# Softmax scaling moved from VectorE to ScalarE, and deferred output products drained two at a time, in an attention and FFN kernel on eight cores

## The reference

```
q_c, q_r = xn @ Wq, rope(xn @ Wqr)          # 16 heads, 64 + 32 features
latent   = xn @ Wkvd                        # 256 features
k_c, v   = latent @ Wku, latent @ Wvu;  k_r = rope(xn @ Wkr)
scores   = [q_c, q_r] . [k_c, k_r] / sqrt(96), causal
e        = exp(scores - m);  attn = e / (sum(e) + exp(lobo_log))
y        = (attn @ v) @ Wo
h        = fix(pwl_gelu(fix(xn @ w1 + b1))) # 4096 features, rounded to 1/256
out      = x + y + fix(h @ w2 + b2)
```

## Time and profile before

| what | value |
|---|---|
| median of 3 runs | 4929.59 us (4919.1 to 4930.2) |
| profiled execution | 4929.35 us |
| its span, slowest core (core 4) | 4927.5 us |
| spans of the eight cores | 4886.9 to 4927.5 us |
| busy: VectorE, TensorE, ScalarE | 50%, 42%, 23% of the span |
| granted TensorE clock, mean | 0.645 of full speed |

### The profile page before, as it was taken

The page is one execution under the profiler, slowest core; times in us unless marked ns, Lnnn a source line. Parts: engine busy times, 40 slices in busy tenths (PEclk is TensorE's granted clock), DMA queues, the critical chain, the costliest instruction groups (busy, mean ns, idle before and its releaser), DMA issues.

```text
span 4927.5 us, 37045 instructions; the slowest of 8 cores (4886.9 to 4927.5 us)
## 1 busy us (share of the span) xinstructions
PE 2056.3 (42%) x7010; PEld 817.0 (17%) x7072; DVE 2455.7 (50%) x4454; ACT 1137.9 (23%) x1957; POOL 386.8 (8%) x352
## 2 busy tenths in 40 slices
PE   0111026035444534444445445455544455454545
PEld 0000002011111111111111122222222222222221
DVE  1222231048755765675582555555555555555551
ACT  1111001011111211111110333333333333333320
POOL 1000000012211211221120000000000000000001
PEclk8555558556676666657655566666666666666668
DMA  5222320942233222222222344444444444444454
GB/s 96 58 58 62 96 62 9 107 73 55 56 73 72 54 66 68 64 57 71 71 56 74 65 81 76 82 77 80 76 82 76 81 77 77 79 81 79 79 91 67
DMA packets 883113, 352.69 MB, mean 72 GB/s; under 512 B 831824, under 2 KB 834384, under 8 KB 882384
## 3 DMA queue, kind: packets, MB, share of 16 engines
q1 hardware_dynamic: 871184, 309.89, 29.8%
q0 software_dynamic: 11712, 40.44, 6.3%
HBM read 174.68 MB, written 41.94 MB: 44 GB/s over the span
## 4 chain that ended last, share of the span: by engine, by line
DMA 31%; DVE 23%; PE 20%; issue 12%; ACT 6%; another core or an unknown queue 3%; SPq 2%; DVEq 1%; ACTq 0%; POOL 0%; POOLq 0%
DMA PT<-Ebuf 10%; DMA W2C<-w2bf 7%; DMA W1C<-w1bf 6%; PE ps L659 6%; DVE u_t L917 6%; PE ps L998 4%; PE ps L631 3%; DMA xtile<-xb 2%; ACT Ebuf L904 2%; DVE Ebuf L948 2%; PE ps L809 2%; PE ps L874 2%; DMA out<-OB 1%; PE ps L496 1%
## 5 line engine op out<-in xcount | busy, mean ns | idle before, releaser
L917 DVE TENSOR_REDUCE u_t<-Ebuf 128x1 f32<-128x1536 bf16 (+3 forms) x480 | 644.8, 1354 | 338.6 <-ACT Ebuf L904 337.8
L904 ACT ACTIVATE Ebuf<-ps 128x1536 bf16<-128x1536 f32 (+3 forms) x480 | 544.8, 1136 | 943.0 <-DVE ps L892 815.2
L659 PE MATMUL ps<-xnTq,W1C 128*128 128x512 bf16 x1006 | 439.7, 612 | 758.7 <-DMA W1C<-w1bf 756.6
L874 PE MATMUL ps<-kasm,qh 96*128 96x512 bf16 (+1 forms) x1152 | 445.7, 499 | 630.2 <-ACT Ebuf L904 609.8
L998 PE MATMUL ps<-PT,vtok 128*64 128x256 bf16 x2304 | 451.2, 381 | 334.8 <-DMA PT<-Ebuf 332.1
L631 PE MATMUL ps<-W2C,HQ 128*128 128x512 bf16 x1001 | 353.6, 496 | 319.3 <-DMA W2C<-w2bf 116.3
L998 PEld LDWEIGHTS ps<-PT,vtok 128*64 128x64 bf16 x2304 | 350.9, 158 | 480.6 <-issue 422.8
L675 ACT ACTIVATE FT<-ps,b1t 128x512 f32<-128x512 f32 x128 | 88.0, 687 | 1458.4 <-PE ps L659 1458.4
L892 DVE TENSOR_TENSOR ps<-ps,m12sb 128x128 f32<-128x128 f32 x512 | 123.8, 288 | 373.9 <-PE ps L874 373.9
L691 DVE TENSOR_SCALAR FT<-FT 128x512 f32<-128x512 f32 x128 | 55.6, 434 | 503.6 <-ACT FT L675 503.3
L659 PEld LDWEIGHTS ps<-xnTq,W1C 128*128 128x128 bf16 x1024 | 130.3, 136 | 1047.0 <-issue 1044.2
(11 more groups left out here) (93 smaller groups left out, 2169.3 us busy)
## 6 DMA issues: line engine op xcount, KB each, us to landing
W2C<-w2bf SPq DMA_DIRECT2D x256, 256.0 KB, 2.8
W1C<-w1bf SPq DMA_DIRECT2D x128, 256.0 KB, 3.4
xtile<-xb SPq DMA_DIRECT2D x32, 512.0 KB, 4.0
xtile<-xq SPq DMA_DIRECT2D x16, 512.0 KB, 4.0
out<-xtile SPq DMA_DIRECT2D x16, 512.0 KB, 3.0
w1bf<-w POOLq DMA_DIRECT2D x8, 1024.0 KB, 48.4
w2bf<-w POOLq DMA_DIRECT2D x8, 1024.0 KB, 122.3
out<-FT POOLq DMA_DIRECT2D x16, 512.0 KB, 5.4
```

What stands on the lines that cost most here:

```text
L659: ins = e.matmul(bkh, W1C[:, fc % 2, dc, :], XNQ[:, dc, tg * 512:(tg + 1) * 512], start=(dc == 0), stop=(dc == 7))
L874: ins = e.matmul(PS[:, (tb + m) * 512:(tb + m) * 512 + wd], QH[0:96, hp, oi * 128:(oi + 1) * 128], KA[0:96, hp, gs + m * 512:gs + m * 512 ...
L904: return e.activation(EB[:, slotE, gs:gs + gl], PS[:, tb * 512:tb * 512 + gl], AF.Exp, scale=SCALE96, accum_out=u_t[:, ub + gi:ub + gi + 1])
L917: ub=ub, gi=gi: e.reduce_max(u_t[:, ub + 3 + gi:ub + 4 + gi], EB[:, slotE, gs:gs + gl], axis=AX.X)),
```

## The change

There are two edits. In the FFN each chunk takes up to two products out of the queue instead of three. In attention the multiplication of a row by its reciprocal leaves VectorE: `fred` ends with the reciprocal and increments a new semaphore `s_fr`, and an Identity activation on ScalarE with the reciprocal as scale does the multiplication. Both rows' activations, and both transposes, are written after all of the pair's exponentials and ahead of the read-out L1007 and of the next pair's exponentials.

```
-            drain_o(3)
+            drain_o(2)
...
-                def fred(e, slotE=slotE, km=km, ng=len(grps), h=h, ub=ub):
+                def fred(e, km=km, ng=len(grps), h=h, ub=ub):
...
-                    vhz(e, e.reciprocal(u_t[:, r8 + 9:r8 + 10],
-                                        u_t[:, r8 + 8:r8 + 9]))
-                    return e.tensor_scalar(EB[:, slotE, 0:km],
-                                           EB[:, slotE, 0:km],
-                                           u_t[:, r8 + 9:r8 + 10], None,
-                                           ALU.mult)
+                    return e.reciprocal(u_t[:, r8 + 9:r8 + 10],
+                                        u_t[:, r8 + 8:r8 + 9])
                 ev("vector", fred, waits=[s_sex, s_gmx] +
...
-                    else []), incs=[(s_red, 1)])
+                    else []), incs=[(s_fr, 1)])
+                rowq.append((slotE, km, ub, s_fr.n))
                 if rr == 0:
                     ev("vector", (lambda e, kmA=KMU[oiA], kmB=KMU[oiB], k=k:
                                   e.memset(EB[:, (2 * k) % 3, kmA:kmB], 0.0)),
...
+            red_rr = []
+            for slotE_, km_, ub_, frn_ in rowq:
+                ev("scalar", (lambda e, slotE=slotE_, km=km_, ub=ub_:
+                              e.activation(EB[:, slotE, 0:km],
+                                           EB[:, slotE, 0:km], AF.Identity,
+                                           scale=u_t[:, ub + 9:ub + 10])),
+                   waits=[(s_fr, frn_)], incs=[(s_red, 1)])
+                red_rr.append(s_red.n)
+            rowq.clear()
...
+            for rr in range(2):
                 ev("sync", (lambda e, rr=rr, K=Kb, k=k, pto=pto: e.dma_start(
                     out=PT[:, pto:pto + K, rr * 128:rr * 128 + 128],
...
-                   waits=[s_red, (sp, sp.n)] +
+                   waits=[(s_red, red_rr[rr]), (sp, sp.n)] +
                    ([(s_pv, pv_pr[k - 2])] if k >= 2 else []),
                    incs=[(sp, 16)])
```

More of the change, by code:

```diff
@@ L216, in build_program @@
     s_gmx = sem("gmx")
+    s_fr = sem("fr")
     s_etp = [sem("etrA", dma=True), sem("etrB", dma=True)]
@@ L794, in build_program @@
     pend_pv = [None]
+    rowq = []
     smm_hd, vtr_hd, pv_hd = {}, {}, {}
@@ L959, in build_program @@
                        incs=[(s_red, 1)])
-                Kb = KMU[oiB] // 128
-                pto = 0 if k % 2 == 0 else 28
-                sp = s_etp[k % 2]
+            red_rr = []
[7 more added lines that the diff above has]
+            rowq.clear()
+            Kb = KMU[oiB] // 128
+            pto = 0 if k % 2 == 0 else 28
+            sp = s_etp[k % 2]
+            for rr in range(2):
                 ev("sync", (lambda e, rr=rr, K=Kb, k=k, pto=pto: e.dma_start(
```

## The result

The changed kernel takes 5195.46 us (median of 8 runs, 5189.77 to 5207.35) against 4929.89 us (8 runs, 4917.05 to 4938.96) in the same comparison: ratio 1.0544, 95% interval 1.0529 to 1.0559, or 266 us slower. The forecast was 5233, the range 5050 to 5330.

A forecast was written before the change was run, and what follows sets the result against it. No attention engine was full; VectorE worked almost unbroken for 101.1 of a head's 127.25 us, and w2 loads on SyncE's queue chained long FFN chunks. 4929.35 + 386 (attention) - 82 (FFN) = 5233 us, range 5050 to 5330.

The forecast's parts named there:

- The walk through a head: Attention, pair by pair with scalings on ScalarE: pair 7 takes 23.5 us instead of 17.68; sixteen heads +386 us.
- the boundary: Between two heads, 26.1 us before: row B's transpose lands 10.0 us after the last scaling instead of 6.9, +3.1.
- The order costs more than the price: Attention: late scalings, queued ahead of exponentials, and late transposes cost more than ScalarE's 2.07 us for the mean row.
- the lost run-ahead: Attention: ScalarE no longer runs the next row's first exponentials while VectorE combines and scales; no separate size.
- the serial transposes: Attention: both transposes of a pair start late, one after the other, 6.1 us each for 3584 columns.
- The lower bound of +13 a head for a cheap activation: Attention with activations at VectorE's price: still about +13 us a head (+208), as successive transposes set row B's start.
- a stall: FFN, wait at emit_foq, two a group: with two products a chunk each costs some 6 us over two chunks.
- nearly neutral: FFN: averaging three-product and one-product chunks gives 12.2 us against 12.0 for two-product chunks, so hardly any gain.
- VectorE's queue as the bound (faster): Rival, attention: VectorE bounds a head, which loses just its VectorE scalings, 12.6 us; 4646 us, chance 0.10.
- The FFN without gain: Rival, FFN: the read-out blocks VectorE for 14 us and the saving is lost again in waits; 5315 us, chance 0.14.
- Table loads: Rival, attention: Identity between exponentials needs table loads, 256 adding 328 us; 5561 us, chance 0.04 shared with the upper price.
- The lower price in attention: Rival: ScalarE's activations at about VectorE's speed, +208 in attention; 5055 us, chance 0.12 shared with milder ordering.

The follow-up runs named there:

- the half-row run: The changed kernel with ScalarE's scaling activation on only the first half of each row's columns, the other half left unscaled: 5073.48 us, ratio 1.0311.

## Why the prediction was right

**The sum.** +386 and -82 were forecast, +304; 266 us were measured, 38 less. The two experiments with one edit each give +364 and -88, so attention was put 22 us too high and the FFN's gain 6 us too low. The other 10 us, 0.2% of the time, lie between the sum of the two single edits and both together; no run explains them.

**The walk through a head.** It held step by step. Pair 7: 23.5 us forecast, 23.8 measured; row B's exponentials free at 9.3, in fact 10.1; both transposes landed 10.0 after the last scaling, in fact 10.2 (3990.64 against 3980.47). For pairs 3 to 6 the walk gave 13.9, 16.8, 18.9 and 21.1; from the ends of row B's scalings in the same head's timeline I read 13.7, 16.9, 19.0 and 20.6. The three small pairs took 27.3 instead of 28.0 and the boundary 28.7 instead of 29.2. The head came out at 150.2 for 151.4, and sixteen times that 1.2 us, 19, is half of what the sum missed. The price on ScalarE, which no row of before showed, was 2.10 us against my 2.07, and at the Trainium skill's figures ("ScalarE: Activation LUTs", "Rules for kernel authors") 2.11. Its rule that multiplications belong on VectorE agrees with both columns of the trace, 3.70 against 1.29 us for 4096 elements, but it isn't the whole reason here: with the multiplications back on VectorE behind all of the pair's exponentials the kernel was slower still.

**What I said of the cause.** "The order costs more than the price" is shown only in part. The order alone is enough: 29.7 us a head for the late place at VectorE's price. But in the changed kernel the shares are not separated: the wait for the landing is worth 5.8 us a head, taking away 43% of ScalarE's price is worth 6.8, and the rest, with the other 57% of that price in it, is open. The sentence behind it named two parts, the lost run-ahead and the serial transposes. The second was right, and 5.8 us is only what the wait for the landing adds: without it row B's transpose still stood behind row A's on SyncE's queue. The first was right as a description and not shown as a cost: the one way of restoring the run-ahead that was tried on ScalarE cost 18 us a head more. The lower bound of +13 a head for a cheap activation was not tested: the half-row run still paid 16.2, and cheaper than half was not tried.

**The FFN.** The direction was right, and the size, 88 for 82, in part by luck: terms inside were off against each other. A two-product chunk took 11.6 us, not 12.0. The chunk of 14.72 that I had picked was a slow one; over groups 1 to 3 of all eight cores the chunks with three products behind chunk 0 average 14.3, and less the 2.71 of a landing that is 11.6. From the chunk before a change to the second one behind it took 32.1 us, not 29.5, so a stall costs 8.9 us over two chunks and not some 6: the read-out is followed by w2 landings and the w1 load, 8.13 us of idle TensorE ahead of chunk 2, where I had allowed part of one landing. Together (26 x 11.61 + 2 x 32.08 = 366 against 371) they make 5 us a group, 15 in all. Of these only 6 show, because the 398.35 us a group that I took for before was that of the slowest core, and the eight cores average 395.7. That the averaging is "nearly neutral" was the real miss: the forecast's sum has 26 x 0.2 x 3 = 16 us for it and 66 for the stalls, and the run with three products and then one gave 39 of the 88.

**The rivals.** VectorE's queue as the bound (faster) fell: relieved of its 201 us of scalings, VectorE waited 455 us longer for exponentials. The FFN without gain fell with the edit alone at 0.9816. Table loads never appeared. The lower price in attention was not the case: 4096 columns took 3.70 us.

## What to carry to other kernels

Moving an operation to an idler engine is a change of order before it is a change of load: ask what is queued behind it there, and when the transfer that waits for it will now start. Where buffers for rows are few, look at the stretch from the last read of a row to the landing of its transfer: here, of what was taken out of that stretch on a mostly idle ScalarE, half came back as time, and putting one exponential into it made the kernel slower. Taking away the wait between two transfers of one queue did not set them side by side here: look how long each one holds the queue that issues it. A wait on "everything issued so far" changes its meaning when code is moved; name the count that is needed.

## What was not expected

Spreading the same products evenly, with the stalls left in place, gave 39 us. The reason that I would give is the order of the queue: as long as a backlog is left, the product that a chunk drains is an old one, whose `HQ` is long written, and once it is gone each product waits for the one just made. The traces bear this out: when three and one alternate the backlog lasts the whole group, and TensorE's waits for `HQ` fall by 39.6 us. In groups 1 to 3 the kernel before has almost all of these waits behind chunk 16, where a chunk drains one product; such a chunk takes 9.8 us on average over the eight cores, and one of the alternating ones 8.9. And with the last product of a head moved behind the next head's first scores, the boundary that took 26 us of each head gave back 16 (127.3 to 111.2 us a head).
